# Making the right half of K behind the second step's scores, in an attention layer bound by TensorE

## What is computed

```python
q = (x @ Wq + bq).reshape(b, h, t, dh)        # 16 heads of 128
k = (x @ Wk + bk).reshape(b, t, h, dh).transpose(0, 2, 3, 1)
v = (x @ Wv + bv).reshape(b, t, h, dh).transpose(0, 2, 1, 3)
logits = jnp.einsum('bhtd,bhds->bhts', q, k) * scale
mask = jnp.triu(jnp.full((t, t), -jnp.inf, dtype=x.dtype), k=1)
weights = jax.nn.softmax(logits + mask, axis=-1)
out = jnp.einsum('bhts,bhsd->bhtd', weights, v)
out = out.transpose(0, 2, 1, 3).reshape(b, t, h * dh)
return out @ Wo + bo
```

## Time and profile before

| what | us |
|---|---|
| median of 3 runs (1228.59 to 1229.51) | 1229.3 |
| the profiled execution | 1229.01 |
| its span, first to last instruction | 1227.2 |
| TensorE products busy | 1213.9 |
| TensorE weight loads busy | 1077.2 |
| VectorE busy | 858.6 |
| ScalarE busy | 746.6 |
| POOL busy | 747.2 |

### The profile page before, as it was taken

One profiled execution on the slowest core, in us unless ns is written; L12 is line 12 of the kernel. 1 busy time (PEld: TensorE's weight loads), 2 busy tenths in 40 slices (PEclk: granted clock), 3 DMA queues, 4 the chain that ended last, 5 costly groups with the idle time before them and its releaser, 6 DMA issues.

```text
span 1227.2 us, 20579 instructions
## 1 busy us (share of the span) xinstructions
PE 1213.9 (99%) x7556; PEld 1077.2 (88%) x7556; DVE 858.6 (70%) x1674; ACT 746.6 (61%) x1548; POOL 747.2 (61%) x796
## 2 busy tenths in 40 slices
PE   9999999999999999999999999999999999999998
PEld 8888888888889898889999988899898889899987
DVE  7777777776677666766677766677666766677775
ACT  6644444444576667666667765676666666666764
POOL 7445555553576767446767772676767446767763
PEclk9999999999999999999999999999999999999999
DMA  7100000000000001110000012010001100000001
GB/s 170 32 7 14 14 14 7 27 1 9 14 13 14 17 23 31 35 31 14 27 14 14 14 31 65 14 48 14 14 27 31 48 1 13 27 14 14 14 6 35
DMA packets 57346, 29.86 MB, mean 24 GB/s; under 512 B 16288, under 2 KB 57248, under 8 KB 57248
## 3 DMA queue, kind: packets, MB, share of 16 engines
q1 hardware_dynamic: 55888, 27.49, 8.1%
q10 hardware_dynamic: 1360, 1.06, 0.3%
HBM read 26.44 MB, written 2.10 MB: 23 GB/s over the span
## 4 chain that ended last, share of the span: by engine, by line
PE 92%; ACT 2%; POOL 2%; DVE 2%; issue 1%; DVEq 0%; ACTq 0%; POOLq 0%
PE ps L41 27%; PE ps L43 27%; PE ps L42 27%; PE ps L1164 10%; PE ps L1026 1%; PE ps L1005 1%; DVE pt_lo L877 1%; POOL probs L736 1%; ACT q_all L413 0%; ACT pt_hi L491 0%; ACT probs L505 0%; ACT wq_hi L403 0%; POOL wq_lo L622 0%; POOL inv_sum L733 0%; DVE probs L958 0%
## 5 line engine op out<-in xcount | busy, mean ns | idle before, releaser
L736 POOL TENSOR_TENSOR probs<-probs,inv_sum 128x128 f32<-128x128 f32 (+7 forms) x256 | 293.6, 1147 | 20.1
L733 POOL TENSOR_TENSOR inv_sum<-row_sum,minus_one 128x1 f32<-128x1 f32 x256 | 140.5, 549 | 225.2 <-ACT probs L505 224.2
L505 ACT ACTIVATE probs<-probs,neg_max 128x128 f32<-128x128 f32 (+7 forms) x256 | 198.8, 777 | 92.2 <-DVE neg_max L958 90.3
L491 ACT ACTIVATE pt_hi<-ps 128x512 fp32r<-128x512 f32 (+3 forms) x384 | 173.7, 488 | 93.0 <-PE ps L1164 90.4
L877 DVE TENSOR_TENSOR pt_lo<-ps,pt_hi 128x512 fp32r<-128x512 f32 (+3 forms) x384 | 200.9, 551 | 16.0 <-ACT pt_hi L491 15.8
L958 DVE CUSTOM_DVE_ANT_0 probs<-ps,mask_row 128x128 f32<-128x128 f32 (+7 forms) x256 | 192.1, 750 | 6.4
L1164 PE MATMUL ps<-ident,probs 128*128 128x128 f32 x1152 | 168.7, 273 | 4.1 <-DVE pt_lo L877 2.1
L717 POOL TENSOR_TENSOR hid_lo<-act_buf,hid_hi 128x512 fp32r<-128x512 f32 x64 | 82.7, 1293 | 139.3 <-ACT hid_hi L445 139.3
L1164 PEld LDWEIGHTS ps<-ident,probs 128*128 128x128 f32 x1152 | 133.7, 141 | 17.4 <-issue 7.2
L43 PE MATMUL ps<-pt_hi,v_lo 128*128 128x512 f32 (+3 forms) x386 | 133.0, 345 | 0.0
L42 PE MATMUL ps<-pt_lo,v_hi 128*128 128x512 f32 (+3 forms) x386 | 132.9, 344 | 0.0
(11 more groups left out here) (154 smaller groups left out, 3377.1 us busy)
## 6 DMA issues: line engine op xcount, KB each, us to landing
wq_in<-in_wq SPq DMA_DIRECT2D x63, 128.0 KB, 2.4
kv_in<-in_wk SPq DMA_DIRECT2D x16, 256.0 KB, 2.6
wo_in<-in_wo SPq DMA_DIRECT2D x32, 128.0 KB, 2.1
kv_in<-in_wv SPq DMA_DIRECT2D x32, 128.0 KB, 2.4
out<-acc SPq DMA_DIRECT2D x7, 256.0 KB, 2.6
acc<-in_x SPq DMA_DIRECT2D x2, 512.0 KB, 5.4
raw<-in_gate SPq DMA_DIRECT2D x16, 64.0 KB, 1.8
raw<-in_up SPq DMA_DIRECT2D x16, 64.0 KB, 2.0
```

Of the source, the lines that this page charges most:

```text
L491: nc.scalar.activation(pt_blocks(pt_hi, i, ch), T[at % 2][:, 0:blocks * P].rearrange("p (a b) -> p a b", b=P), ACT.Copy).then_inc(pt_hi_do ...
L505: nc.scalar.activation(row, row, ACT.Exp, bias=neg_max[:, s % 16:s % 16 + 1], scale=-1.0, accum_out=row_sum[:, s % 16:s % 16 + 1]).then_in ...
L733: nc.gpsimd.tensor_tensor(inv_sum[:, at], row_sum[:, at], minus_one[:], ALU.pow).then_inc(inv_done, 1)
L736: nc.gpsimd.tensor_tensor(row, row, inv_sum[:, at].to_broadcast([P, (tile_of(h, i) + 1) * P]), ALU.mult).then_inc(probs_done, 1)
```

## The change

The job K1 moves from FIRST to EARLY in step 1, in both tables. Heads 1 to 30 take it from these tables (head 0 has a row of its own, which had K1 at EARLY already, and head 31 makes its K1 in head 30).

```diff
-        EVEN = {0: {EARLY: "K0"}, 1: {FIRST: "K1"}, 2: {EARLY: "O0a"}, 3: {LATE: "O0b"}, 4: {EARLY: "V0", LATE: "V1"},
+        EVEN = {0: {EARLY: "K0"}, 1: {EARLY: "K1"}, 2: {EARLY: "O0a"}, 3: {LATE: "O0b"}, 4: {EARLY: "V0", LATE: "V1"},
                 6: {FIRST: "O1a"}, 7: {FIRST: "O1b"}}
-        ODD = {0: {EARLY: "V2"}, 1: {FIRST: "K1"}, 2: {EARLY: "V3"}, 3: {LATE: "O0a"}, 4: {EARLY: "O0b", LATE: "K0"},
+        ODD = {0: {EARLY: "V2"}, 1: {EARLY: "K1"}, 2: {EARLY: "V3"}, 3: {LATE: "O0a"}, 4: {EARLY: "O0b", LATE: "K0"},
                6: {FIRST: "O1a"}, 7: {FIRST: "O1b"}}
```

## The result

| | before | changed |
|---|---|---|
| median, us | 1229.15 (4 runs, 1228.59 to 1229.51) | 1235.3 (4 runs, 1235.27 to 1235.52) |
| profiled execution, us | 1229.01 | 1235.32 |
| its span, us | 1227.2 | 1233.5 |

The change makes the kernel slower: ratio 1.005, 95% interval 1.0038 to 1.0062, or 6.2 us by the medians. The forecast was 1235.9 with a range of 1233.0 to 1238.6.

The account below looks back on a forecast made before the run. TensorE, 99% busy, was taken as the bound, with the next job waiting for K1's bank. Terms 1.6 + 3.9 + 1.1 = 6.6 us on 1229.0 make 1235.6; the median's 0.3 more gives 1235.9, range 1233.0 to 1238.6.

Parts of the forecast that it names:

- Step 1: Heads 1 to 30: the maximum of scores(1), now earlier, fills VectorE's idle 0.35 before K1's low half; gain 0.
- step 3: Twelve plain even heads: T0's existing 0.22 wait takes up most of the delay; +0.13 a head, 1.6 us.
- Step 2: K1's products end later, so its read-out and the next job's first load, waiting for K1's bank, move by 0.355.
- Step 4: Eleven odd heads with V3 next: no wait absorbs the delay, T0 moves by the whole 0.355; 3.9 us.
- Step 5: Heads 6, 14, 22: ScalarE's chain through the Wq conversions hangs on K1's end; T0 moves 0.355 each, 1.1 us.
- Step 6: Heads 7, 15, 23 covered by two Q steps; head 1 has no job in step 2; cost 0.
- The signs: Trace: load 0.05 after K1's low half, T0 0.12 behind O0a, pt_lo mostly not its releaser, distances growing 0.355 or 0.13.
- The sum: Delays of plain even heads, odd heads and heads 6, 14, 22: 1.6 + 3.9 + 1.1 = 6.6 us.
- C: Slower still: ScalarE's later pt_hi makes pt_lo hold T0 by 0.355 in even heads too; 1238.5 us, chance 0.05.
- D: TensorE's clock falls to 1.2 GHz for one head's length: up to +25.9 us, some 1262; chance 0.02.
- A: Faster: K1's evacuation does not slip, pt_lo starts sooner and T0's 0.22 wait goes; -3.6 us, 1225.7, chance 0.04.
- B: No change: something other than K1's bank holds O0a and V3, or a later wait absorbs the shift; 1229.3, chance 0.04.

## Why the prediction was right, point by point

- **What bounds.** TensorE, and the wait for K1's bank as the place where a slip counts. The 26 waits for `k_lo_right` and the kernels with a bank of K1's own show it.
- **Step 1** (the earlier maximum gains nothing by itself): true for the sum, and worth more than I said. With VectorE's old order the change would have cost 2.6 us more by the medians. I had used that order in step 3 without naming it as something that protects.
- **Step 2** (0.355): against scores(2), ScalarE's start of K1 moved by 0.355 in the mean of the 26 heads (0.35 in head 12), and the next job's load came 0.05 behind VectorE's end in each. Measured at the distance, 0.354 in odd heads.
- **Step 3** (0.13 in plain even heads): mechanism right, size off. T0 itself moved by 0.11 to 0.14, but the distance to the next scores grew by 0.092 only, 1.1 us instead of 1.6. When T0 had waited, the next product started 0.06 behind it (654.49, 654.55 in head 12 before); when it had not, 0.03 (657.14, 657.17). The wait that went had cost 0.03 more than its own length, and the step had no term for it.
- **Step 4** (11 x 0.355 = 3.9): 3.9.
- **Step 5** (3 x 0.355 = 1.1): 1.0, and the wait at V0 moved along, as forecast.
- **Step 6** (no cost in 7, 15, 23 and 1): none.
- **The signs.** All came, but for one that could not be read as it was put: `pt_lo` was to be no longer named as the releaser of T0 in plain even heads, and PE's list had never named it there. The weight loads' list and T0's distances show what the sign was for.
- **The sum** was 6.6, the distances give 6.0, the medians 6.2. Almost all of the difference is step 3. The chances leave a small slip: forecast, C and D, all slower, add up to 0.92, and the text gives 0.90. Of the rivals, A failed on its condition, since the load came later; B on the same point and on the kernels with a bank of K1's own; C on T0 standing 0.12 behind O0a; D on the clock, which is 1.00 from 366 to 1184 us with all the new waits in it. On that last point the rule that the prediction took from the Trainium skill ("TensorE: Matmul & The Clock Gate", section "A second HAM failure mode: psum-queue depth-cycling") is not borne out by this trace.

Left open are differences in what no edit touched. In the profiled executions the first part of the program took from 0.3 less to 1.0 more than before, and the stretches behind scores(3) that hang on none of the waits above from about the same to 1.0 less in all. So gains of a microsecond, as with K1's own bank on the kernel before, rest on the distances in the heads, which repeat to about 0.02, more than on the medians.

## What to carry to other kernels

Before moving a group of products later, look for who next writes the bank that it fills: where only 0.05 lies between the read-out's end and the next job's first load, every tenth of slip is paid, however idle the engines that read it out. The same slip costs nothing in a bank of its own, unless something else that TensorE waits for stands behind the read-out in an engine's list, as in heads 6, 14 and 22. A wait behind the slipped work absorbs part of it; so price heads, tiles or stages by kind, not by a mean. And a gain at one wait is only paid out if the engine behind the next wait keeps up.

## What the runs showed of the hardware

Listed waits of TensorE understate and busy shares hide. In the 26 heads the last product of the job of step 2 comes 0.41 to 0.45 later in the changed kernel than in the one with the own bank and the later read-out, 11.0 us in all; PE's list gives 4.2 for it. Of the 11.0, 2.0 was there before the change, 3.0 is taken up by the waits of T0 that went, and 6.0 remain. The kernel before lost 0.08 in each of 11 heads at a place that no view lists. Starts of weight loads show it: a load that follows VectorE's end by 0.05 in every head is a load that waited.
